# From batch 2 on, x is loaded by blocks of 32 features, scaled by GpSimd and turned by VectorE

## The reference

```python
# attention, 16 heads of 32
scale, shift = split(cond @ W_emb + b_emb)            # per batch and feature
xn  = rms_norm(x) * g_norm * (1 + scale) + shift      # rms over the 512 features of a row
q, k, v = heads(xn @ W_qkv);  q, k = rms_norm(q) * g_q, rms_norm(k) * g_k
o   = softmax(q k^T / sqrt(32)) v
x1  = x + o + o @ W_out
# GRU cell over the 256 rows, one after the other; its state starts as cond
r, z = sigmoid(i_r + h_r), sigmoid(i_z + h_z);  n = tanh(i_n + r * h_n)
h   = (1 - z) * n + z * h;   out = x1 + h
```

## Time and profile before

| | |
|---|---|
| median of three runs | 1731.39 us |
| the profiled execution: its time, its span | 1732.12 us, 1730.3 us |
| busy, share of the span | PE 98%, PEld 79%, DVE 65%, ACT 57%, POOL 22% |
| PE groups in the attention | L468 360 x 3 products, L545 1024, L526, L560, L507; L455 128 transposes, 272 ns mean, 18.8 us busy |
| granted TensorE clock, mean | 0.997 |
| DMA | 127.78 MB, 212123 packets, 16 engines busy 30% with queue 1 |

### The profile page before, as it was taken

How to read it: one execution, slowest core, us unless ns; L and a number is a source line. 1 busy time by engine, 2 the same in 40 slices (tenths; PEclk the granted TensorE clock), 3 DMA queues, 4 the chain that set the end, 5 groups by cost and what they waited for, 6 DMA issues and landing times.

```text
span 1730.3 us, 68496 instructions
## 1 busy us (share of the span) xinstructions
PE 1694.1 (98%) x28787; PEld 1374.2 (79%) x28787; DVE 1127.0 (65%) x4057; ACT 981.5 (57%) x3592; POOL 388.0 (22%) x480
## 2 busy tenths in 40 slices
PE   8999999999999999999999999999999999999986
PEld 6788888888888887678888888888888888888864
DVE  5767777666777777366666666666666666666655
ACT  5777777777777777144444444444444444444444
POOL 4533333333334333011111111111111111111111
PEclk9999999999999999999999999999999999999999
DMA  6032222222212215642333333333333333332320
GB/s 232 12 124 50 60 56 52 50 50 50 50 50 50 50 38 125 124 84 72 82 79 81 82 73 83 80 78 82 75 79 80 75 80 82 82 81 68 73 67 14
DMA packets 212123, 127.78 MB, mean 74 GB/s; under 512 B 79116, under 2 KB 193496, under 8 KB 211816
## 3 DMA queue, kind: packets, MB, share of 16 engines
q1 hardware_dynamic: 211776, 123.39, 29.8%
q10 hardware_dynamic: 40, 0.01, 0.0%
HBM read 73.01 MB, written 50.33 MB: 71 GB/s over the span
## 4 chain that ended last, share of the span: by engine, by line
PE 94%; DVE 2%; ACT 1%; issue 1%; DMA 1%; POOL 0%; SPq 0%; POOLq 0%; DVEq 0%; ACTq 0%
PE ps L727 38%; PE ps L698 19%; PE ps L468 14%; PE ps L545 7%; PE ps L581 5%; PE ps L526 4%; PE ps L560 4%; PE ps L507 2%; PE ps L568 1%; PE ps L455 1%; DMA wstage<-in_L_cond_W_qkv_dram 1%; ACT P L1112 0%; DVE nmx L795 0%; DVE v L992 0%; DVE v L997 0%
## 5 line engine op out<-in xcount | busy, mean ns | idle before, releaser
L727 PE MATMUL ps<-whh,hT 128*32 128x192 f32 x16384 | 719.6, 326 | 16.7 <-DVE hT L1018 16.1
L727 PEld LDWEIGHTS ps<-whh,hT 128*32 128x32 f32 x16384 | 579.5, 110 | 132.0 <-DVE hT L1018 80.3
L1231 ACT ACTIVATE v<-ps 128x128 f32<-128x128 f32 x512 | 139.2, 272 | 438.1 <-PE ps L727 438.1
L698 PE MATMUL ps<-wih,x1T 128*32 128x256 f32 x6144 | 382.3, 379 | 0.7 <-ACT x1T L1131 0.7
L1348 POOL TENSOR_TENSOR outG<-hG,GI 128x128 f32<-128x128 f32 x256 | 116.8, 456 | 916.3 <-DVE hG L1011 916.3
L992 DVE SCALAR_TENSOR_TENSOR v<-v,ps 128x64 f32<-128x64 f32 x512 | 113.1, 221 | 276.4 <-ACT v L1231 276.4
L698 PEld LDWEIGHTS ps<-wih,x1T 128*32 128x32 f32 x6144 | 236.6, 110 | 70.2 <-ACT x1T L1131 0.9
L1112 ACT ACTIVATE P<-ps,nmx 128x256 f32<-128x256 f32 x496 | 229.0, 482 | 0.0
L1239 ACT ACTIVATE v<-v 128x64 f32<-128x64 f32 x512 | 131.3, 256 | 106.5 <-DVE v L997 106.5
L1287 POOL TENSOR_TENSOR rq<-msq,mh 128x16 f32<-128x16 f32 x64 | 185.8, 2904 | 5.4 <-POOL msq L1283 0.2
L795 DVE TENSOR_REDUCE nmx<-ps 128x4 f32<-128x1024 f32 x128 | 156.2, 1221 | 27.5 <-PE ps L526 27.5
(11 more groups left out here) (111 smaller groups left out, 1996.9 us busy)
## 6 DMA issues: line engine op xcount, KB each, us to landing
gscr<-nat SPq DMA_DIRECT2D x96, 256.0 KB, 2.8
GI<-gscr SPq DMA_DIRECT2D x128, 192.0 KB, 3.7
xb<-in_x_dram SPq DMA_DIRECT2D x16, 512.0 KB, 3.6
xres<-in_x_dram SPq DMA_DIRECT2D x32, 256.0 KB, 3.0
xscr<-x1s SPq DMA_DIRECT2D x32, 256.0 KB, 2.0
xblk<-x1s SPq DMA_DIRECT2D x128, 64.0 KB, 2.7
GI<-xscr SPq DMA_DIRECT2D x128, 64.0 KB, 2.7
out_dram<-outG SPq DMA_DIRECT2D x128, 64.0 KB, 2.9
```

What stands on the lines that cost most here:

```text
L698: last = pe.matmul(F[G % 2][q, n], x1T[:, tt % 2, j, c, :], wih[:, c, g * D + 256 * half:g * D + 256 * half + 256], start=(c == 0), stop=( ...
L727: last = pe.matmul(ps[32 * j:32 * j + 32, q, 0:192], hT[:, 32 * c:32 * c + 32], whg[:, c, :, 128 * j + 64 * q:128 * j + 64 * q + 64], star ...
L1231: s.activation(v_rz[:, q, :], ps[:, q, 64:192], ACT.Tanh, scale=0.5).then_inc(s_tr, 1)
```

## The change

For batches 2 to 15 the "rows" pieces are gone. x comes by 16 DMAs of 32 partitions with runs of 32 features (128 B), so that partition 32a + t holds, for eight row blocks r and four chunks c, the features 128c + 32a to 128c + 32a + 31 of row 32r + t. ScalarE squares all 1024 columns at once; VectorE sums the 128 squares of each block r (`x_sums`, w=1). A row's total lies over four partitions; one product with a matrix of ones at equal positions modulo 32 ("sums", end of w=1, bank 7) adds them. VectorE makes mean + eps (`x_mean`, w=2), GpSimd the power -0.5 over 128x8 and the scaling of the whole block (`scale_blocks`), and VectorE turns it by 32x32 blocks in one transpose (`turn_x`, end of w=2). `affine` reads SBUF now. GpSimd builds the matrix `Gs` in the prologue, by four small instructions.

```diff
-    rows = ("rows", m, v - 2) if m < NB and v > 1 else None
+    sums = ("sums", m) if m < NB else None
...
-        [(("project", n, 0, 0), ("turn", n, 0, 1), None), (("out", b - 1, 1) if b else None, ("turn", n, 1, 1), None)],
-        [(("project", n, 1, 0), ("turn", n, 0, 0), None), (("project", n, 0, 2), None, rows)],
-        [(("project", n, 1, 2) if m < NB else None, None, rows), (("out", b, 0), ("turn", n, 1, 0), None)],
+        [(("project", n, 0, 0), ("turn", n, 0, 1), None), (("out", b - 1, 1) if b else None, ("turn", n, 1, 1), sums)],
+        [(("project", n, 1, 0), ("turn", n, 0, 0), None), (("project", n, 0, 2), None, None)],
+        [(("project", n, 1, 2) if m < NB else None, None, None), (("out", b, 0), ("turn", n, 1, 0), None)],
...
@@ sync, load_x: b < 2 as before; then
+                if b == 2:
+                    sp.wait_ge(s_xT, 4)
+                else:
+                    sp.wait_ge(s_xt, b - 2)
+                for a in range(4):
+                    for c in range(KC):
+                        f = 128 * c + 32 * a
+                        sp.dma_start(xq[32 * a:32 * a + 32, :].rearrange("p (r c k) -> p r c k", r=8, c=KC)[:, :, c, :],
+                                     x[b, :, f:f + 32].rearrange("(r t) k -> t r k", r=8)).then_inc(s_x, 16)
@@ tensor
+            def sums(m, bank):
+                if m == 2:
+                    pe.wait_ge(s_gs, 4)
+                pe.wait_ge(s_ssp, m - 1)
+                pe.matmul(ps[:, bank, 0:8], Gs, ssp, start=True, stop=True).then_inc(s_sums, 1)
@@ vector
+            def x_sums(m):
+                v.wait_ge(s_xsq, m - 1)
+                v.tensor_reduce(ssp, sqx, AXX, ALU.add).then_inc(s_ssp, 1)
+            def x_mean(m):
+                v.wait_ge(s_sums, m - 1)
+                if m > 2:
+                    v.wait_ge(s_rx, m + 2)
+                v.tensor_scalar(msp, ps[:, BANK["sums", m], 0:8], 1.0 / D, EPS, ALU.mult, ALU.add).then_inc(s_ev[BANK["sums", m]], 1)
+            def turn_x(m):
+                v.wait_ge(s_xs2, m - 1)
+                v.transpose(xt, xq).then_inc(s_xt, 1)
+            def affine(b, half):
+                r = xt.rearrange("p (r c t) -> p c r t", r=8, c=KC)
+                v.wait_ge(s_xt, b - 1)
+                v.wait_ge(s_xlo, 2 * b + half - 1)
+                for k in range(2):
+                    c = 2 * half + k
+                    done = v.tensor_scalar(xf[:, k, :].rearrange("p (r t) -> p r t", r=8), r[:, c], Aff[:, c, b:b + 1], Shf[:, c, b:b + 1],
+                                           ALU.mult, ALU.add)
+                done.then_inc(s_xa, 1)
...
                 if p:
                     scale(p - 1)
+                if w == 2 and m < NB:
+                    x_mean(m)
...
-                if w == 2 and m < NB:
-                    x_scale(m)
+                if w == 1 and m < NB:
+                    x_sums(m)
                 keep_turned_p(2 * p + 1)
...
                 if w == 2 and m < NB:
-                    affine(m, 0, BANK["rows", m, 0])
+                    turn_x(m)
+                    affine(m, 0)
@@ scalar
+            def square_blocks(m):
+                s.wait_ge(s_x, 32 + 256 * (m - 1))
+                if m == 2:
+                    s.wait_ge(s_wsd, 3 * KC)
+                else:
+                    s.wait_ge(s_ssp, m - 2)
+                s.activation(sqx, xq.rearrange("p (r f) -> p r f", r=8), ACT.Square).then_inc(s_xsq, 1)
...
-                    if w < 2:
-                        square(m, w)
+                    if w == 0:
+                        square_blocks(m)
@@ gpsimd
+            def scale_blocks(m):
+                emptied(g_, ("sums", m))
+                g_.tensor_tensor(rxp, msp, mh[:, 0:8], ALU.pow).then_inc(s_rx, 1)
+                g_.wait_ge(s_rx, m + 3)
+                xv = xq.rearrange("p (r f) -> p r f", r=8)
+                g_.tensor_tensor(xv, xv, rxp.unsqueeze(2).to_broadcast([128, 8, 128]), ALU.mult).then_inc(s_xs2, 1)
...
                 rsqrt(n, 0, 0)
                 if m < NB:
-                    rsqrt_x(m)
+                    scale_blocks(m)
                 rsqrt(n, 1, 0)
```

More of the change, by code:

```diff
@@ L114, in cond_resid_kernel @@
         mh = sb("mh", [128, NH])
+        Gt = sb("Gt", [128, 32])
+        Gs = sb("Gs", [128, 128])
+        ssp, msp, rxp = (sb(n, [128, 8]) for n in ("ssp", "msp", "rxp"))
         nmx = sb("nmx", [128, 2, 4, 2])
@@ L126, in cond_resid_kernel @@
         P = sb("P", [128, 4, 4, T])
+        sqx = sb("sqx", [128, 8, 128])
+        xt = sb("xt", [128, 2 * D])
+        assert base[0] <= a_wi + 4 * KC * 3 * D
         base[0] = a_wi + 4 * KC * 3 * D
@@ L135, in cond_resid_kernel @@
         xb = sb("xb", [128, 2, D])
+        xq = xb.rearrange("p i d -> p (i d)")
         raw = sb("raw", [128, 2, D])
@@ L230, in cond_resid_kernel @@
         s_ev = {k: sem(f"bank{k}_empty") for k in (6, 7)}
+        s_gs, s_xsq, s_ssp, s_sums, s_xs2, s_xt, s_xa = (
+            sem(n) for n in ("ones_by_32", "x_block_squares", "x_block_sums", "x_sums", "x_block_scaled", "x_blocks_turned", "x_block_affine"))
         s_qk0 = [sem("q_kept0"), sem("k_kept0")]
@@ L259, in load_x @@
             def load_x(b):
-                if b:
-                    sp.wait_ge(s_xT, 2 * b)
-                sp.dma_start(xb, x[b].rearrange("(i p) d -> p i d", p=128)).then_inc(s_x, 16)
+                if b < 2:
+                    if b:
+                        sp.wait_ge(s_xT, 2 * b)
+                    sp.dma_start(xb, x[b].rearrange("(i p) d -> p i d", p=128)).then_inc(s_x, 16)
+                    return
+                if b == 2:
[7 more added lines that the diff above has]
+                                     x[b, :, f:f + 32].rearrange("(r t) k -> t r k", r=8)).then_inc(s_x, 16)
             def load_residual(b, i):
@@ L638, in passed @@
                     x_transpose(*a, BANK[piece])
+                elif kind == "sums":
+                    sums(*a, BANK[piece])
                 else:
@@ L740, in x_scale, with first_affine @@
                     v.tensor_scalar(xb[:, i, :], xb[:, i, :], rx[:, i:i + 1], None, ALU.mult).then_inc(s_xs, 1)
-            def affine(b, half, bank):
+            def first_affine(half, bank):
                 r = ps[:, bank, :].rearrange("p (c t) -> p c t", c=2)
[L744 to L747, removed]
+                v.wait_ge(s_xT, half + 1)
                 for k in range(2):
                     c = 2 * half + k
-                    if b == 0 and c == 0:
+                    if c == 0:
                         v.wait_ge(s_aff, 3)
[L752 to L756, removed]
+                    v.tensor_scalar((xf, xf1)[half][:, k, :], r[:, k, :], Aff[:, c, 0:1], Shf[:, c, 0:1], ALU.mult,
+                                    ALU.add).then_inc(s_xn, 1)
+            def x_sums(m):
[18 more added lines that the diff above has]
+                done.then_inc(s_xa, 1)
             def squares(b, i, g):
@@ L878, in _ @@
                                    op0=ALU.add, op1=ALU.mult).then_inc(s_aff, 1)
-            affine(0, 0, 0)
-            affine(0, 1, 1)
+            first_affine(0, 0)
+            first_affine(1, 1)
             x_low(1)
@@ L957, in _ @@
                 if w == 3 and m < NB:
-                    affine(m, 1, BANK["rows", m, 1])
+                    affine(m, 1)
                 if p + 1 < NP:
@@ L1048, in square @@
                 s.activation(xsq, xb[:, i, :], ACT.Square, accum_out=ssx[:, i:i + 1]).then_inc(s_ssx, 1)
+            def square_blocks(m):
[5 more added lines that the diff above has]
+                s.activation(sqx, xq.rearrange("p (r f) -> p r f", r=8), ACT.Square).then_inc(s_xsq, 1)
             def x_high(b, half):
                 h = slice(2 * half, 2 * half + 2)
-                if (b, half) == (1, 1):
+                if b > 1:
+                    s.wait_ge(s_xa, 2 * (b - 2) + half + 1)
+                    s.wait_ge(s_qkv, 6 * (b - 1))
+                elif half:
                     s.wait_ge(s_r11, 1)
                 else:
-                    emptied(s, ("rows", b, half))
-                if b > 1:
-                    s.wait_ge(s_qkv, 6 * (b - 1))
+                    emptied(s, ("rows", 1, 0))
                 s.copy(xh[b % 2][:, h, :], xf1 if b < 2 and half else xf).then_inc(s_xh, 1)
@@ L1301, in _ @@
             rsqrt_x(0)
+            g_.tensor_tensor(Gt, ident[:, 0:32], ident[:, 32:64], ALU.add).then_inc(s_gs, 1)
+            g_.wait_ge(s_gs, 1)
+            g_.tensor_tensor(Gt, Gt, ident[:, 64:96], ALU.add).then_inc(s_gs, 1)
+            g_.wait_ge(s_gs, 2)
+            g_.tensor_tensor(Gt, Gt, ident[:, 96:128], ALU.add).then_inc(s_gs, 1)
+            g_.wait_ge(s_gs, 3)
+            g_.tensor_copy(Gs.rearrange("p (a k) -> p a k", a=4), Gt.unsqueeze(1).to_broadcast([128, 4, 32])).then_inc(s_gs, 1)
             x_low(0, 0)
```

## The result

Four runs of the changed kernel took 1741.63, 1741.70, 1742.88 and 1746.32 us, median 1742.29, against 1731.29 for the kernel before (four runs). The ratio is 1.0071, 95% interval 1.0059 to 1.0084: slower by 11.0 us. Forecast were 1747 and a range of 1727 to 1760; the likeliest case's own range was 1741 to 1756.

A forecast was written before the change was run, and what follows sets the result against it. TensorE was taken as the bound, 94% of the chain of waits. 14 x (-0.28) = -3.9, 13 x 1.4 = +18.2 and +1.7 for the first batch gave +16.0 us, so 1747, range 1727 to 1760.

The forecast's parts named there:

- the likeliest case: GpSimd's product blocks VectorE's normalize of q in w=2, stalling TensorE 1.0 to 1.8 us; 1741 to 1756, chance 0.60.
- two rows pieces removed: TensorE, end of w=2 and in w=3: two pieces of four transposes leave each batch, -0.86 us.
- product with ones and its wait: TensorE, end of w=1: 0.23 us product plus a wait for ScalarE's copy from bank 7, +0.33 us a batch.
- transpose in front of `scale`: VectorE, end of w=2: turn_x and affines delay scale, which TensorE awaits in w=3; +0.25 us, between 0 and 0.7.
- `normalize` blocked, turn late: w=2: VectorE's normalize of q waits for GpSimd's product, delaying TensorE's turn; +1.4 us a batch, between 0 and 1.9.
- start of the product in w=2: GpSimd's product over 128x1024 starts 2.54 us into the pass, 0.4 before normalize is due at 2.95.
- its length: GpSimd's product over 128x1024 in w=2 takes 2.5 us, twice the 128x512 subtraction's 1.272.
- The first batch: New reduction in front of the already late P copy, +1.1 us once, and 0.6 for its w=2; +1.7 together.
- B: w=2: GpSimd's product comes second or lets VectorE in between, so normalize is on time; 1728.5, 1724 to 1731, chance 0.21.
- C: Neither the port block nor turn_x reaches TensorE, the GpSimd or VectorE instructions being shorter; -6.3 us, 1725, chance 0.09.
- D: Stall long enough to drop TensorE's clock, a batch losing 5 us; +65, 1797, chance 0.07.
- E: x load late, 16 DMAs above 1.2 us each, costing ScalarE one microsecond each batch; 1761, chance 0.03.

The follow-up runs named there:

- e1: Changed kernel, with GpSimd's product over 128x1024 waiting until VectorE's normalize of q of the same pass is done; 1731.89 us, ratio to before 1.0006.
- e3: Changed kernel, with turn_x moved from the end of w=2 to x_scale's old place, before the second P copy; 1738.62 us, ratio to before 1.0047.
- e4: Changed kernel without the product with ones, so x_mean reads the partial sums from SBUF; 1737.80 us, ratio to before 1.0042.
- e2: Changed kernel, with GpSimd's product over 128x1024 issued as two over 128x512 at the same place; 1732.07 us, ratio to before 1.0009.
- e5: Kernel before plus a GpSimd pow over 128x4 and product over 128x1024 on an unread tile, in 13 batches; 1741.09 us, ratio 1.0058.
- e6: Kernel before, with x of batches 2 to 15 loaded by the change's 16 DMAs and handled as before; 1730.51 us, ratio 0.9999.
- e8: Changed kernel, with the product with ones moved into w=2 right behind scores; 1732.02 us, ratio to before 1.0011.
- e7: Changed kernel: GpSimd's product behind normalize, turn_x at x_scale's place, product with ones behind w=2's scores, x_sums behind w=1's P copy and squares; 1722.82 us, 0.9953.
- e9: e7 plus batch 0's four GpSimd wo_l subtractions of 128x512 issued as sixteen of 128x128; 1723.48 us, ratio to before 0.9959.

## Why the prediction was right, and where its sizes were off

The likeliest case happened: the sign, the mechanism and the place. By its steps, per batch, forecast against measured:

| step | forecast | measured | shown by |
|---|---|---|---|
| two rows pieces removed | -0.86 | -0.79 | e1's w=2, 10.23 (192.87 to 203.10) for 10.66, and e3's w=3, 10.27 for 10.63 |
| product with ones and its wait | +0.33 | +0.37 | e4 |
| transpose in front of `scale` | +0.25 | +0.39 | e3 |
| `normalize` blocked, turn late | +1.4 | +0.79 | e1, e2, e5 |
| square, x load, x_scale | 0 | 0 (w=0: +0.04, cause not tried) | e6 for the load |
| pow of 128x8 | 1.64 us | 1.638 | the groups of the page after |
| start of the product in w=2 | 2.54 | 2.50 | the rows above |
| its length | 2.5 us | 1.90 | the rows above |

**The mis-sized term** is the length of the product over 128x1024. I took twice the subtraction of 128x512, 1.272, and allowed only for a slower one. It takes 1.90; whether that is because its second operand is eight repeated values a row was not tried. So the stall is 0.61 shorter, 13 times, 7.9 us. The first batch is 0.6 shorter too (next paragraph). Against that stand four small ones, each 14 times: the transpose in front of `scale` (`turn_x` 1.24, not 1.2, the affines 0.74 the pair, not 0.6) 0.14 more, 2.0 us; 0.07 less gained by the removed pieces, 1.0; 0.04 for the product with ones, 0.6; 0.04 in w=0, 0.6. 16.0 - 7.9 - 0.6 + 4.2 is 11.7; measured 11.0. The stall of 0.79 lies under the 1.0 to 1.8 that the likeliest case allowed. That 1742.3 is still inside its 1741 to 1756 is in part luck: the small terms came out larger and made up for some of it.

**The first batch** I put at +1.7: 1.1 for the new reduction in front of the P copy in w=1, and 0.6 for w=2. The first part can be read; in the changed kernel TensorE runs `turn` at 60.17 and then has:

```profile
63.99 0.36 PE L657 MATMUL ps<-ssp,Gs 128*128 128x8 f32 x2 [3.19 <-DVE ssp L785]
64.58 1.12 PE L582 MATMUL ps<-PT,V 128*32 128x128 f32 x32 [0.24 <-DVE PT L859]
```

From `turn` to `times_v` it is 4.41 us, and 3.28 in the kernel before (60.38 to 63.66): +1.13. The second part is a toss-up that the order of two starts decides:

```profile
69.98 0.68 DVE L819 TENSOR_TENSOR raw<-raw,rq 128x512 f32<-128x512 f32 x1
...
69.99 2.43 POOL L1339 TENSOR_TENSOR xb<-xb,rxp 128x1024 f32<-128x1024 f32 x1
```

VectorE is first by 0.01 us, and `turn` there has no wait; in e3 GpSimd is first (70.04 against 70.13), and it waits 0.97. e1's total agrees with the first part: its batch is 0.02 shorter than the old one (14 times, 0.2), and it is still 1.06 above the kernel before. In e7, with `x_sums` behind the P copy, the wait there is back to 2.66. What these parts do to the total is blurred by the clock, for the reason in the last section.

**The rivals.** B (the product second) and C did not happen, but e8 shows B's point: the product 0.96 us later than in the changed kernel, and the order turns. I had given B 0.4 us of margin, and it was 0.45. D did not happen: the stall is 0.8. E is refuted by e6: the load costs nothing. Its 16 DMAs take SP 7.74 us to issue and not 12: I had scaled from DMAs with twice the bytes, and from a slow instance; the other issues of those four in the steady part before take 2.13 us at the least and mostly under 2.4, where row 8 has 3.00. The Trainium skill ("SBUF — State Buffer", Who interferes with whom) says "whole instruction", and that the first to issue blocks the other, in its sentence on VectorE's 2-port modes; for two SBUF inputs it says that they contend. For the latter e2 and e8 agree with both: one instruction, and whoever starts first.

## What to carry to other kernels

Where one engine is full, a step given to an idle one is free only if it shares nothing with the engines that feed the full one: here one product a batch on GpSimd, 25% busy, cost some 10 us, because VectorE's two-input instruction had to wait for its end, and the full engine for that. Look up the start of each long GpSimd instruction against VectorE's next instruction that somebody waits for, if it has two operands in SBUF or is a cast from SBUF to SBUF (both were blocked here); one `wait_ge` puts GpSimd's behind it. And when a piece leaves the full engine, look at each neighbour's waits again: they come due earlier by what was gained.

## What the runs showed of the hardware

A power of 128x16 on GpSimd (2.90 us) blocks nothing that these traces show. A product or a subtraction over 512 or 1024 columns blocks VectorE's two-operand instruction in SBUF until its end (1.99 and 1.69 us in the place of 0.68), and its cast from SBUF to SBUF too (1.14 in the place of 0.28, e1). Reductions and copies that read PSUM are not blocked (1.22 and 0.68 us beside a product), and neither was a reduction that reads SBUF (1.21 us for 1024 columns beside e9's subtractions).

TensorE's clock after one and the same idle time is not the same in each execution. The earlier trace rows have 2.65 us and then 5.6 us at 0.50, the 1.2 GHz level. e5_before_product and e7_all have 2.66 us at the same place and none of it. The changed kernel and e1, the same up to there, both wait 3.2 us, and from 60 to 80 us their mean granted clock is 0.91 and 0.83. The timeline and the stretch behind it in e7_all, whose last columns are PEclk, DMA share and GB/s:

```profile
63.58 1.08 PE L583 MATMUL ps<-PT,V 128*32 128x128 f32 x32 [2.66 <-DVE PT L862]
```
```profile
63.60:69.20 5.60, 5.60 (x70) 4.61 (x71) 5.40 (x10) 2.77 (x10) 5.29 (x5) 1.00 0.00 0
```

The first batch, the same work for TensorE in both, lasted 45.41 us with the drop in the kernel before (`scores` 43.34 to 88.75) and 42.63 without it in e5_before_product (43.07 to 85.70). So an idle time of that length is a draw for some 2.8 us. The 57 runs of the kernel before in the three groups spread over 4.5 us, 1728.0 to 1732.6, and go with the clock: the 12 with a mean clock of 0.999 took 1729.6 us in the mean, the 9 with 0.997 took 1731.5. What decides the draw these runs do not show.
